# Second attention's projections placed between the chunks of the first feed-forward, with its outputs spread over the next group

## The reference

```python
def _L0_ffn_ref(x, fast_b, w_fc, w_proj, u, v, gate):
    h = _bitlinear(x, w_fc) + gate * (x @ v.T @ fast_b.T @ u.T)
    r = jnp.maximum(h, 0.0)
    return _bitlinear(r * r, w_proj)

def _L1_xattn_ref(x, ctx, Wq, Wkv, Wproj, q_gamma, k_gamma):
    q = (x @ Wq).reshape(B, L, H, hd).transpose(0, 2, 1, 3)
    kv = (ctx @ Wkv).reshape(B, Lc, 2, H, hd).transpose(2, 0, 3, 1, 4)
    k, v = (kv[0], kv[1])
    q = _rmsnorm(q, q_gamma)
    k = _rmsnorm(k, k_gamma)
    ...
x = x + jnp.tanh(g_xattn[0]) * _L0_xattn_ref(_layernorm(x, axis=-1), ...)
x = x + jnp.tanh(g_ffn[0]) * _L0_ffn_ref(_layernorm(x, axis=-1), ...)
x = x + jnp.tanh(g_xattn[1]) * _L1_xattn_ref(_layernorm(x, axis=-1), ctx_1024, ...)
x = x + jnp.tanh(g_ffn[1]) * _L1_ffn_ref(_layernorm(x, axis=-1), ...)
```

## Time and profile before

| what | value |
|---|---|
| median of 3 runs | 1161.57 us (1159.33 to 1162.9) |
| the profiled execution, its own time | 1160.38 us |
| its span, first to last instruction | 1158.5 us |
| mean granted TensorE clock, share of full speed | 0.925 |
| PE busy | 958.8 us, 83% of the span |
| DVE busy | 822.9 us, 71% |
| ACT busy | 683.9 us, 59% |
| POOL busy | 712.6 us, 62% |

### The profile page before, as it was taken

One profiled execution on the slowest core, in us unless ns is written; L12 is line 12 of the kernel. 1 busy time (PEld: TensorE's weight loads), 2 busy tenths in 40 slices (PEclk: granted clock), 3 DMA queues, 4 the chain that ended last, 5 costly groups with the idle time before them and its releaser, 6 DMA issues.

```text
span 1158.5 us, 32871 instructions
## 1 busy us (share of the span) xinstructions
PE 958.8 (83%) x12178; PEld 778.2 (67%) x12178; DVE 822.9 (71%) x1947; ACT 683.9 (59%) x1338; POOL 712.6 (62%) x811
## 2 busy tenths in 40 slices
PE   0549999999999974679878469993899999999996
PEld 0346777777777753445554358871799999999995
DVE  3988887788778867468777689966566566666663
ACT  2457888888888863065426368864354444444452
POOL 2988888876776672034512569974566666666672
PEclk9878999999999997589989679985899999999998
DMA  9276776787677755500001000002553225832251
GB/s 285 66 197 138 137 143 157 161 194 151 153 155 143 135 121 137 187 7 1 1 26 44 5 2 21 21 21 92 170 156 94 32 45 166 259 88 32 31 143 14
DMA packets 52117, 119.65 MB, mean 103 GB/s; under 512 B 7616, under 2 KB 30144, under 8 KB 51632
## 3 DMA queue, kind: packets, MB, share of 16 engines
q0 software_dynamic: 14144, 35.48, 21.3%
q1 hardware_dynamic: 35520, 80.71, 20.5%
q10 hardware_dynamic: 2352, 2.10, 0.6%
HBM read 212.54 MB, written 37.85 MB: 216 GB/s over the span
## 4 chain that ended last, share of the span: by engine, by line
PE 51%; DVE 17%; POOL 11%; ACT 9%; issue 6%; DMA 4%; ACTq 0%; SPq 0%; POOLq 0%; DVEq 0%
PE bank L2107 17%; PE bank L2121 9%; POOL PT L560 5%; PE bank L1786 5%; PE bank L1689 3%; ACT EX L1393 2%; PE bank L1728 2%; PE bank L1766 2%; DVE h L1063 2%; DVE nmx L1177 2%; PE bank L1937 2%; ACT L1362 1%; PE bank L1721 1%; PE bank L1899 1%; ACT fks L1362 1%
## 5 line engine op out<-in xcount | busy, mean ns | idle before, releaser
L1623 ACT ACTIVATE yg<-bank,bms 128x128 f32<-128x128 f32 x312 | 105.7, 363 | 113.1 <-PE bank L2107 106.0
L1296 DVE TENSOR_TENSOR hm<-hf,hm 128x256 f16<-128x256 f32 x156 | 66.8, 428 | 99.7 <-ACT hm L1630 94.2
L2107 PE MATMUL bank<-xT,wm_even 128*128 128x128 f16 x1920 | 117.7, 221 | 3.1 <-DVE hf L1291 1.8
L1291 DVE SCALAR_TENSOR_TENSOR hf<-bank,bms,yg 128x128 f32<-128x128 f32 x312 | 98.6, 346 | 26.9 <-ACT yg L1623 25.8
L707 POOL DMA_INDIRECT out_x<-ys,sidx x39 | 62.7, 1608 | 86.2 <-DVE ys L1310 86.2
L2107 PEld LDWEIGHTS bank<-xT,wm_even 128*128 128x128 f16 x1920 | 111.5, 99 | 6.2 <-DVE hf L1291 3.9
L2107 PE MATMUL bank<-xT,wm_odd 128*128 128x128 f16 x1824 | 110.1, 219 | 2.3 <-DVE hf L1291 2.3
L2107 PEld LDWEIGHTS bank<-xT,wm_odd 128*128 128x128 f16 x1824 | 104.2, 98 | 4.9 <-DVE hf L1291 2.4
L1630 ACT ACTIVATE hm<-hf 128x256 f16<-128x256 f32 x156 | 64.6, 414 | 69.0 <-DVE hf L1291 68.2
L560 POOL TENSOR_TENSOR PT<-PT 128x512 f16<-128x512 f32 x64 | 72.3, 1158 | 42.7 <-ACT PT L1419 42.7
L619 POOL TENSOR_TENSOR h<-h 128x512 f16<-128x512 f32 x32 | 40.6, 1281 | 81.8 <-DVE h L1063 79.8
(11 more groups left out here) (308 smaller groups left out, 2658.7 us busy)
## 6 DMA issues: line engine op xcount, KB each, us to landing
wm_even<-expert_weights SPq DMA_DIRECT2D x60, 1024.0 KB
wm_odd<-expert_weights SPq DMA_DIRECT2D x57, 1024.0 KB
expert_weights<-in_wcat POOLq DMA_DIRECT2D x16, 768.0 KB, 8.0
wsp<-expert_weights SPq DMA_DIRECT2D x16, 768.0 KB, 4.3
wsp<-in_wcat POOLq DMA_DIRECT2D x16, 768.0 KB, 10.8
expert_weights<-wsp SPq DMA_DIRECT2D x16, 768.0 KB, 3.3
Lst<-gate_tables SPq DMA_DIRECT2D x48, 68.0 KB, 5.9
gate_tables<-Lw SPq DMA_DIRECT2D x6, 512.0 KB, 4.6
```

Of the source, the lines that this page charges most:

```text
L1291: v.scalar_tensor_tensor(hf[:, (c // 2) % 2, c % 2, :], bank[c % 4][:, MT:2 * MT], bms[:, par, FC + c:FC + c + 1], yg[:, c % 4, :], ALU.ad ...
L1296: v.tensor_tensor(hm16[:, par, 1, c - 1:c + 1, :], hf[:, q % 2, :, :], hm16[:, par, 0, c - 1:c + 1, :], ALU.subtract).then_inc(m_hl, 1)
L1623: s.activation(yg[:, c % 4, :], bank[c % 4][:, 0:MT], ACT.Gelu, bias=bms[:, par, c:c + 1]).then_inc(m_g, 1)
L2107: ins = t.matmul(bank[c % 4][:, w * MT:(w + 1) * MT], wm16[par][:, wp, col:col + P], xT16[:, par, xp * KD + kk, :], start=(n == 0), stop=( ...
```

## The change

Nothing of the arithmetic's amount changes, apart from one operand. What changes is the order, on all five engines. The 32 chunks become 32 slots (`n`), and other work is written between them:

- Keys and values of tile n stand behind the hidden chunk n, in slots 0 to 15 (`project1(n, 1)`), with `ctx_high1(n + 1)`, `split_ctx1(n + 1)`, `key_value(n - 1)`, `key_squares(n - 1)` and `copy_raw(n - 1, 1)` on the other engines. `key_gamma` goes to POOL's slots 16 to 31.
- The outputs of group g - 1 stand one by one in slots 1 to 4 of group g, their residuals on DVE one slot later. In slot 5 of a group DVE has the variances of its predecessor's four tiles, ACT the root, and in slot 6 DVE makes `rstd` of those four.
- Queries (`turn1`, `project1(b, 0)`): tiles 0 to 3 are turned in slots 17 to 20, tiles 4 to 7 in slots 23 to 26, tile 8 in slot 31, each projected a slot later. Tiles 9 to 15 come in a tail behind slot 31, together with the last group's four outputs; the last four tiles' statistics are made in two halves (12 and 13, then 14 and 15).
- A hidden chunk has two PSUM banks in place of four (0 and 1), the outputs have banks 6 and 2, and the projections 7 and 3, a whole bank for a tile. The chunk n waits for DVE's square of chunk n - 2 too, since DVE reads that bank now: the square is `bank * hr` in place of `hr * hr`.
- The projection weights are split before slot 0 (ACT ahead of `ffn_high(0)`, DVE ahead of its first square), and 32 small memsets become two.
- POOL's 11 constants and SP's loads of `rwt`, `bma` and `b2a` wait for the last residual (`f_xu` at 16). SP starts the first two context loads ahead of the projection weights, the others as their buffers come free.
- Six buffers of the projections (20 KB of a partition) are allocated below the feed-forward's buffers and not above them.

The diff, cut to its core:

```diff
+def query_at(n):
+    for first, b, count in ((2 * FC + 1, 0, GT), (3 * FC - 1, GT, GT), (4 * FC - 1, 2 * GT, 2)):
+        if first <= n < first + count:
+            return b + n - first
+    return None
...
+                    if n + 1 < B:
+                        split_ctx1(n + 1, (n + 1) % 2)
                     gp.wait_ge(f_sq, n + 1)
                     gp.wait_ge(f_h2, n + 1)
...
+                    if n >= B:
+                        key_gamma(n - B)
+
+            gp.wait_ge(f_xu, B)
...
-                    v.tensor_tensor(h2[:, n % 2, :], hr[:, n % 2, :], hr[:, n % 2, :], ALU.mult).then_inc(f_h2, 1)
+                v.scalar_tensor_tensor(h2[:, n % 2, :], bank[n % 2][:, :], 1.0 / WSC, hr[:, n % 2, :], ALU.mult, ALU.mult).then_inc(f_h2, 1)
...
+                    if 0 < n <= B:
+                        key_value(n - 1)
+                    ffn_square(n)
+                    if c < GT and g + 2 < NG:
+                        ffn_norm(g + 2, c)
+                    if g and c == 6:
+                        make_rstd(b0, b0 + GT)
+                    if g and 2 <= c < 2 + GT:
+                        ffn_residual(b0 + c - 2)
+                    if g and c == 5:
+                        tile_variance(b0, b0 + GT)
+                    if 0 < n <= B:
+                        key_squares(n - 1)
+                    if c == 4 and g + 1 < NG:
+                        ffn_low(g + 1)
+                    if query_at(n) is not None:
+                        low1(query_at(n))
+                    if query_at(n + 1) is not None:
+                        norm1(query_at(n + 1))
+                    if query_at(n - 1) is not None:
+                        query_squares(query_at(n - 1))
...
+                    if n + 1 < B:
+                        ctx_high1(n + 1)
+                    ffn_relu(n)
+                    if 0 < n <= B:
+                        copy_raw(n - 1, 1)
+                    if g and c == 5:
+                        root(g + 2, (g - 1) * GT, g * GT)
+                    if query_at(n) is not None:
+                        high1(query_at(n))
+                    if query_at(n - 1) is not None:
+                        copy_raw(query_at(n - 1), 0)
...
+                    ffn_hidden(g, c)
...
+                    if n < B:
+                        project1(n, 1)
+                    if query_at(n - 1) is not None:
+                        project1(query_at(n - 1), 0)
+                    if query_at(n) is not None:
+                        if query_at(n) == 0:
+                            pe.wait_ge(a_raw, B)
+                            pe.wait_ge(a_v, 2 * B)
+                        turn1(query_at(n))
+                    if g and 1 <= c < 1 + GT:
+                        ffn_out((g - 1) * GT + c - 1)
```

More of the change, by code:

```diff
@@ L1484, in ffn_relu @@
+            ac.wait_ge(a_ld, 80)
+            s.activation(w1_16[:, 0, :, :], wst1[:, :, :], ACT.Copy, scale=WSC).then_inc(a_w, 1)
+            ffn_high(0)
+            ctx_high1(0)
+            for g in range(NG):
+                if g + 1 < NG:
+                    ffn_high(g + 1)
                 for c in range(FC):
                     n = g * FC + c
-                    ac.wait_ge(f_h, n + 1)
-                    if n > 1:
-                        ac.wait_ge(f_sq, n - 1)
-                        ac.wait_ge(f_h2, n - 1)
@@ new lines, in _ @@
+                    if g and c == 5:
[4 more added lines that the diff above has]
+                        copy_raw(query_at(n - 1), 0)
+            b0 = (NG - 1) * GT
+            for b in range(b0 - 3, b0):
+                high1(b)
+                copy_raw(b - 1, 0)
+            root(NG + 2, b0, b0 + 2)
+            copy_raw(b0 - 1, 0)
@@ L1546, in _ @@
+            high1(b0)
+            high1(b0 + 1)
+            root(NG + 3, b0 + 2, b0 + 4)
+            copy_raw(b0, 0)
+            copy_raw(b0 + 1, 0)
+            high1(b0 + 2)
+            high1(b0 + 3)
+            copy_raw(b0 + 2, 0)
+            copy_raw(b0 + 3, 0)
             ac.wait_ge(a_ms, 1)
@@ new lines, in ffn_out @@
+            def ffn_out(n):
+                g, i = n // GT, n % GT
+                if i == 0:
+                    pe.wait_ge(f_l, FC * (g + 1))
+                if n > 1:
+                    pe.wait_ge(f_ot, n - 1)
+                for m in range(2 * FC):
+                    ins = t.matmul(bank[6 - n % 2 * 4][:, 0:D], h216[:, g % 2, m // FC, m % FC, i * N:(i + 1) * N], W2T16[:, m % FC, :],
+                                   start=(m == 0), stop=(m == 2 * FC - 1), skip_group_check=True)
+                ins.then_inc(f_o, 1)
@@ new lines, in turn1, with project1 @@
+            def turn1(b):
+                pe.wait_ge(s_xn, B + b + 1)
+                if b > 1:
+                    pe.wait_ge(a_rq, b - 1)
+                for kk in range(KD):
+                    ins = t.transpose(bank[7 - b % 2 * 4][:, kk * N:(kk + 1) * N], xn1[:, b % 2, kk * P:(kk + 1) * P], ident[:, :])
+                ins.then_inc(s_xt, 1)
+            def project1(b, w):
+                if w:
+                    pe.wait_ge(s_ch, b + (B + 1))
+                    pe.wait_ge(s_cl, b + (B + 1))
+                    if b > 1:
+                        pe.wait_ge(a_raw, b - 1)
+                        pe.wait_ge(a_v, 2 * b - 2)
+                    src, dst, c0, c1, done = c116, bank[7 - b % 2 * 4][:, :], D, 3 * D, a_kf
+                else:
+                    pe.wait_ge(s_xh, B + b + 1)
+                    pe.wait_ge(s_xl, B + b + 1)
+                    src, dst, c0, c1, done = x116, bank[7 - b % 2 * 4][:, D:], 0, D, a_qf
+                n = 0
+                for (wp, xp) in PAIRS:
+                    for kk in range(KD):
+                        ins = t.matmul(dst, src[:, b % 2, xp, kk, :], w1_16[:, wp, kk, c0:c1], start=(n == 0), stop=(n == 5), skip_group_check=True)
+                        n += 1
+                ins.then_inc(done, 1)
```

439 lines of the change are left out of this document (199 added, 240 removed).

## The result

The changed kernel took 1146.59 us (median of 4 runs, 1143.62 to 1148.27) against 1160.45 (4 runs) of the kernel before: ratio 0.9877 [0.9847, 0.9907]. A second pair, taken later with more runs, gave 1140.62 against 1152.88 us, ratio 0.9906 [0.9884, 0.9928]. The unchanged kernel alone lies 7.6 us apart in the two pairs, so times are compared only within a pair. The change is faster by 0.9 to 1.2%, and the forecast of 1147 lies on the median of the first pair. The sum behind it does not hold as well, as the stretch that it was made for shows.

The account below looks back on a forecast made before the run. PE was taken as the bound, idle 36.2 of 153.4 us. Groups, tail and clock: 21.0 + 29.7 + 27.6 + 26.0 + 22.5 + 3.7 = 130.5 against 144.5 us; with 0.5, gain 14.5: 1147, range 1139 to 1157.

Parts of the forecast that it names:

- Group 0, keys and values behind hidden chunks: Slots 0 to 7: PE bounds them with eight hidden chunks and eight tiles' keys and values, 21.0 us.
- rival 2: Context loads set the slot, 3.1 us per slot, 7 us more: 1154 (1152 to 1158); chance 0.19.
- Groups 1, 2 and 3: Slots 8 to 31: PE's work plus waits, forecast as 29.7, 27.6 and 26.0 us.
- residual held by POOL, I take 0.4: DVE's residuals in slots 2 to 5: 1.31 us each, up to 0.72 more where POOL holds them, taken as 0.4.
- `rstd` 1.5: DVE's `rstd` in slot 6 of a group: 1.5 us, estimated from the earlier statistics stage.
- the 4.5: Group 2, slot 4 to the turn of tile 4: waits on DVE and ACT add 4.5 us to PE's 23.1.
- Clock: 3.7: PE at half speed after pauses: 1.65 us twice for groups 2 and 3, 0.4 for the tail, and group 0's slow start.
- Tail: Behind slot 31: PE's work up to the last output, 12.2 us, then a chain of 10.3; together 22.5 us.
- The gamma products: POOL's 16 products moved into slots 16 to 31: 0.5 us gained before the first attention turn.
- The square: DVE's square reading PSUM and one SBUF operand: taken as 0.64 us, the other end being the old square's 1.64.
- rival 3: POOL still holds the new square, 1.64 us in place of 0.64: 22 us more, 1169; chance 0.07.
- Rival 4: Queues wait so often for the two banks that a slot costs the sum of its parts: 1161; chance 0.05.

Follow-up runs that it names:

- `gamma_behind`: The changed kernel with POOL's 16 gamma products back behind the last tile; stretch 146.68 us, 3.6 us more than the changed kernel.

## Why the prediction was right, and where its steps failed

**The direction and the size.** The gain was forecast as 14.5 us; the runs give 10.8 to 14 (ratios of 0.9906 and 0.9877), and the stretch itself 10.3. That 1147 was met to 0.4 us is luck: the time outside the stretch was 6.6 us shorter in the first pair's profiles, which no term of the sum has. With the 10.3 us alone the forecast would have been 1151, still inside the range. One of my signs of being wrong, that the stages outside change their lengths, did come up; as two profiles of one and the same kernel lie 7.0 us apart there, it says little about the mechanism.

**Group 0, keys and values behind hidden chunks: right.** 21.8 us from the first hidden matmul to the next group's turn; 21.0 was the sum, and 0.8 is the slow start of the first chunk. ACT's context part never waited for DMA, so rival 2 did not come in.

**Groups 1, 2 and 3: the waits were under-priced.** Group 1 took 30.7 us for 29.7, group 2 30.6 for 27.6, group 3 29.1 for 26.0. The step "residual held by POOL, I take 0.4" failed: it was 0.73 for ten of the twelve in the groups (1.21 for 0.48) and 0.45 for the first two, and nothing in the tail. I had averaged over the cases of the earlier trace rows, but POOL's subtraction is released by the square just ahead of the residual, so it falls on the update each time, whole or in part. "`rstd` 1.5" was an estimate from the earlier trace rows and took 2.3 (607.66 to 609.95), since the next subtraction and a gamma product hold it. In group 1 PE waited 1.94 us for ACT's copy. In group 2 the 4.5 stood for all that lies between the start of slot 4 and T(4), and so for two waits, 1.14 ahead of P(3) and 4.73 ahead of T(4). From that start to the end of T(4), 566.93 to 582.05, it took 15.1 us for the forecast 13.9: P(3) ended at 7.2 (6.9), the variances at 9.9 (9.3), `rstd` at 14.1 (13.0). The rest of the excess of 3.0 is the wait of 1.87 ahead of T(0), which was in no sum. With the residual ahead of the square, group 1 was 2.1 us and group 2 3.3 us shorter (from hidden chunk to hidden chunk 28.6 and 26.3, for 30.7 and 29.7), so these waits hung on DVE's order there.

**Clock: 3.7 was too little.** The sum names a slow start of group 0, but 1.65 twice and 0.4 are already 3.7, so it stood at nothing. Summed from the rows at half speed the clock cost about 5.8: 0.8 at the start, some 2.3 behind T(4) (2.77 for 1.46, 1.49 for 0.82, and two turns) and some 2.6 behind T(8). I had taken the 1.65 of the earlier trace rows as the price of a pause, but it is a price per pause and place, and it was larger here.

**Tail: nearly right.** 23.6 us for 22.5, some 2.2 of clock in it. The last sum came at 634.66 (forecast 633.5), the first attention turn at 642.07 (642), but these two agree by luck: the stretch began 4.1 us earlier than in the kernel before. Counted from its start the last sum came at 135.7 us for 130.5. The loads that wait for the last residual, put at 4.9 us at most, were longer in the kernel before (`b2a` 7.3 us from issue to landing); the first attention turn did not wait for them.

**The gamma products: right in kind, too small.** I counted 0.5; behind the last sum 8.99 us became 7.41, 1.6 less. In the old order moving them shortens that part by 2.1 (8.98 to 6.86). The error was to look at POOL's end alone: DVE's small steps were held as well, 0.41, 0.70, 0.63 and 0.71 us before, 0.29, 0.29, 0.23 and 0.29 after, and so was the scaling of the first tiles, 2.14 and 1.28. Nor did I count what they cost at the knots, 0.5 us each.

**The square: right value, wrong reason for its worth.** 690 ns for the forecast 0.64. But rival 3, which I priced at 22 us, was priced as if a square that can be held is held: with the SBUF operand back the stretch was 0.7 us longer, or 1.6 with the clock. What decides is whether POOL's subtraction runs beside it, and the new order had already moved it away: beside none of the 32. By the rule on who interferes with whom in the Trainium skill's SBUF — State Buffer two SBUF inputs make a DVE instruction open to POOL; the traces agree for the update of X and for the old square, and add that 735 ns against 1136 is a matter of what stands beside it.

**Rival 4, that the interleaving gains nothing,** got 0.05. It was false as put, but it had more in it than I saw: the operand alone in the old order does as much as the whole change. I had compared the change with the kernel before, not with its cheapest part.

## What to carry to other kernels

When two engines hold each other, look first at which instruction is released by which: the one that always follows the release is held every time, and an average over the cases underprices it. Before an order is rebuilt, try its smallest part alone, here one operand; two edits that cure the same loss do not add. Work that is put between other work to fill an engine can also keep its clock up, and a long pause that the new order leaves can cost more than its own length: behind 4.73 and 5.21 us the half speed cost another 2.3 and 2.6, behind 1.87 and 1.14 us nothing. And a single profile can hide a gain or feign one by its clock: compare the pauses, and then whole runs.

## What the runs showed of the hardware

The same elementwise instruction with two SBUF inputs of 512 f32 columns took 0.69 us alone and 1.64 beside a POOL subtraction that began 0.1 us ahead of it. With one of them in PSUM its mean was 0.69 in both orders. That form is another operation (SCALAR_TENSOR_TENSOR), but the operation is not the cure: the update of X has it too, with both tensors in SBUF, and was held. Instructions of four columns can be held as long as one of 256: 1.00 us in place of 0.16. Even one with a single SBUF tensor was, 0.65 us for 0.17 beside a gamma product, and a norm from SBUF to SBUF took 0.96 for 0.41 beside the gamma products (`gamma_behind`).

PE's granted clock does not follow the pause alone: behind the same pause of 2.66 us in the tail, four profiles have all later query products at full speed (0.81 us for six matmuls), one has them at half speed (1.44), and in four more the clock fell at the product behind the first.
